# Inputs and output laid out by feature on the host, and a shorter path from the recurrence to the first expert product, in a recurrent mixture-of-experts kernel

## The chip, the cores and the metric

One core of one Trainium2 chip. The metric is the device time of one execution in microseconds (us), the median over the executions shown; lower is better. The profile comes from one further execution of the same program.

## The reference

`x` has the shape (32, 32, 128): 32 rows of 32 time steps with 128 features. A recurrent layer with tanh runs over the 32 steps, and a routed feed-forward layer with 16 experts, top 4 of them per token, works on its states:

```python
xw = einsum('ntd,dh->nth', x, Wx) + b
h_t = tanh(xw_t + h_{t-1} @ Wh)                    # h_0 = cond_1024, 32 steps in series
xn = h * rsqrt(mean(h * h) + 1e-5) * norm_scale
vals, idx = top_k(xn @ wg + bg, 4); gates = softmax(vals), spread to 16 columns
u = xn @ w1[e] + b1[e]                             # (1024 tokens) x 256, for each of 16 experts
s = min(u[::2], 7) * sigmoid(1.702 * min(u[::2], 7)) * (clip(u[1::2], -7, 7) + 1)
out = x + h + sum_e gates[:, e] * (s @ w2[e] + b2[e])
```

## The kernel before, in words

All work runs with features on partitions and tokens in columns. The 1,024 tokens are 8 tiles of 128 columns; a tile is 4 time steps of 32 rows. The tiles form three chunks of 2, 2 and 4 tiles. The experts' work is cut into 32 units: 8 units of 2 experts for chunk 0, 8 such units for chunk 1, 16 units of one expert for chunk 2. A unit has 512 columns of result per half. Order is written out by hand: each engine has its own instruction stream, and semaphores join the streams.

**A unit** (`for v in range(NU)` in every stream). TensorE computes the half `a` into `psA` and the half `b` into `psB` (`up`, L849). Each expert's product has three passes: rounded weights by rounded input (`w1_hi`, `xn_hi`), the weights' rounding rest by rounded input (`w1_lo`, `xn_hi`), and rounded weights by the input's rest (`w1_hi`, `xn_lo`). ScalarE takes `psA` through two activations (L527, L536), VectorE takes `psB` into `lin` (L726) and forms `act` (L741), GpSimd multiplies by the gates (L440), and TensorE adds `w2`'s product four units later (`down`, L878).

**The recurrence** is spread through the same streams. Eight steps form the head, ahead of unit 0; the other 24 run two to a unit in units 0 to 11. Step t is a matmul by `wh_sb` (L798) on top of the product of `x` and `wx` already in PSUM (`x_wx`, L790), then a tanh on ScalarE (L476). The next step waits for it.

**Normalise.** For each group of tiles ScalarE squares (L489), TensorE sums (L805), GpSimd takes the power (L394), TensorE lays the result over the partitions (`lay_rstd`, L820), and VectorE multiplies into `xn` (L587), rounds it to `xn_hi` (L590) and, in the head's two groups, subtracts for `xn_lo` (L594). Then the gates are worked out on VectorE and GpSimd (L610 to L656), turned on TensorE (L838), written to DRAM and read back over all partitions (L339, L345).

**Layout.** `x` comes in with its 32 rows on partitions, `cond` and the two vectors as rows. TensorE transposes them (L779, L917), `b1` as well (L940), and VectorE copies each result out of PSUM (L681 to L686, L697, L745). Tiles 4 to 7 of `x` are transposed in unit 2. At the end of each chunk the result `yT` is transposed back (L901, L911), copied out (L499, L548, L551, L766) and stored in pieces of 32 partitions (L312, L351).

**Fillers.** `keep_warm` (L827) issues matmuls on constants: seven of 512 columns at the start, and some of 256 columns later.

ScalarE also rounds the weights `w1` (L484) in the head from step 2 on and in units 0 to 2; VectorE (L669) and GpSimd (L423) form the rests.

Of the kernel before, what the change touches and what calls it, by code (L numbers as in the profile page):

```python
# [15 lines left out]
def adaln_rnn_moe_kernel(nc, x, cond, wx, wh, b, norm_scale, wg, bg, w1, b1, w2, b2, out):  # L16
# [7 lines left out]
    N, T, D = x.shape  # L24
    E, H, I2 = w1.shape
# [5 lines left out]
    NT = N * T // P  # L31
# [10 lines left out]
    WARM, WARM_START, WARM_GAP = 512, 7, 256  # L42
# [7 lines left out]
    XW_TILES = W // P  # L50
# [12 lines left out]
    ROWS_OUT = [UNIT0[c + 1] + LAG + 2 for c in range(NC - 1)] + [None]  # L63
# [6 lines left out]
    with ctx:  # L70
# [10 lines left out]
        rows = sb("rows", [N + 2, D])  # L81
        wx_sb = sb("wx_sb", [D, H])
        wh_sb = sb("wh_sb", [H, H])
        x_sb = sb("x_sb", [N, T, D])
        b1_sb = sb("b1_sb", [E, I2])
        wg_sb = sb("wg_sb", [H, E])
        bg_sb = sb("bg_sb", [P, E])
        b2_sb = sb("b2_sb", [E, H])
        w1_sb = sb("w1_sb", [H, E, I2])
# [11 lines left out]
        b_col = sb("b_col", [P, 2])  # L101
# [4 lines left out]

        xT = sb("xT", [D, NT * P])
        hT = sb("hT", [H, (T + 1) * N])
# [27 lines left out]
        y_sb = sb("y_sb", [P, NT, D])  # L136
# [5 lines left out]
        rows_loaded = sem("rows_loaded")  # L142
        x0_loaded = sem("x0_loaded")
        x1_loaded = sem("x1_loaded")
        x_loaded = sem("x_loaded")
        wx_loaded = sem("wx_loaded")
        wh_loaded = sem("wh_loaded")
        b1_loaded = sem("b1_loaded")
        wg_loaded = sem("wg_loaded")
# [6 lines left out]
        x_t = sem("x_t")  # L156
        xT_ready = sem("xT_ready")
# [21 lines left out]
        x_mm = sem("x_mm")  # L179
        x_read = sem("x_read")  # L180
# [11 lines left out]
        out_mm = sem("out_mm")  # L192
        rows_ready = sem("rows_ready")
        last_rows = sem("last_rows")
# [5 lines left out]

        out_v = out.rearrange("n (j s) d -> s n j d", s=TL)
        w1_v = w1.rearrange("e h i -> h e i")
        w2_v = w2.rearrange("e i h -> i e h")
# [75 lines left out]
        def xw_bank(j):  # L279

            return psY if j in (0, 2) else psR

        def step_psum(t):

            k = t % (TL * XW_TILES)
            return xw_bank(t // TL)[:, k * N:(k + 1) * N]
# [4 lines left out]
        def psM_turn(what):  # L291

            order = ["rows", "b1"] + [(k, g) for g in range(last_group(0) + 1) for k in ("stats", "rstd")]
# [7 lines left out]
        def psX_turn(what):  # L301

# [12 lines left out]
        def _(sp):  # L315
# [32 lines left out]
            def store_rows(c):  # L348

                for s in range(TL):  # L350
                    sp.dma_start(out_v[s][:, tiles(c), :], y_sb[s * N:(s + 1) * N, tiles(c), :]).then_inc(stored, 16)  # L351
# [676 lines left out]
```

## Time and profile before

| | |
|---|---|
| median of three executions | 113.96 us (113.69 to 113.98) |
| profiled execution: its time, its span | 113.94 us, 112.1 us |
| busy share of TensorE, VectorE, ScalarE, GpSimd | 95%, 59%, 56%, 57% |
| the chain that ended last, by engine | TensorE 84%, VectorE 10%, ScalarE 2% |
| DMA traffic | 12.96 MB, mean 116 GB/s |

The span runs from the first to the last instruction; the 1.84 us between it and the time lie around it. The chain is followed back from the last instruction: at each step to what released it, or to the instruction before it on its engine. So its shares say on which engine time was spent where nothing else could have ended the kernel earlier.

### The profile page before, as it was taken

The page shows a single profiled execution, that of the slowest core. Times are in us where ns is not written, and L with a number is a line of the kernel's source. Part 1 is how long each engine was busy: PE and PEld are TensorE (multiplying, and loading weights), DVE is VectorE, ACT ScalarE, POOL GpSimd, SP SyncE. Part 2 cuts the span into 40 slices and gives each one's busy share as a digit, 9 for nine tenths or more (in the row PEclk, how much of TensorE's full clock was granted, in tenths as well). Part 3 has the DMA queues.
Part 4 walks back from the last instruction along what each step waited for, and adds up shares of the span by engine and source line. Part 5 has one row for each costly group of instructions (what it writes and reads, how often), then busy time and mean ns, then how long its engine had stood idle before and what let it go on. Part 6 is the DMA issues. An engine that isn't in the chain of part 4 may idle for free.

```text
span 112.1 us, 1830 instructions
## 1 busy us (share of the span) xinstructions
PE 106.6 (95%) x600; PEld 90.7 (81%) x600; DVE 66.5 (59%) x180; ACT 62.7 (56%) x143; POOL 64.4 (57%) x76
## 2 busy tenths in 40 slices
PE   7999999999999999999999979999999999999970
PEld 2478978999889999999989968886888888888840
DVE  0110359876735996389756995668265566656720
ACT  4026582998736668567715756654455665466120
POOL 3002444996790698729980799795444575466000
PEclk9999999999999999999999999999999999999999
DMA  1699992007950000992059605990001000000002
GB/s 31 154 268 237 318 303 67 6 9 152 368 231 0 0 6 6 275 371 105 12 129 348 272 6 118 310 368 5 0 0 47 3 0 0 0 0 6 0 23 70
DMA packets 8781, 12.96 MB, mean 116 GB/s; under 512 B 1122, under 2 KB 6628, under 8 KB 8740
## 3 DMA queue, kind: packets, MB, share of 16 engines
q1 hardware_dynamic: 8608, 12.77, 36.4%
q10 hardware_dynamic: 164, 0.07, 0.3%
q8 instruction: 5, 0.08, 0.3%
q14 instruction: 4, 0.03, 0.1%
HBM read 12.25 MB, written 0.59 MB: 114 GB/s over the span
## 4 chain that ended last, share of the span: by engine, by line
PE 84%; DVE 10%; ACT 2%; issue 1%; DVEq 0%
PE psA L849 19%; PE psB L849 18%; PE psY L878 10%; PE psR L878 5%; PE psM L878 5%; PE psR L798 4%; PE psA L827 3%; PE psY L798 2%; PE psB L779 2%; PE psM L805 2%; PE psR L890 2%; PE psM L890 2%; DVE lin L726 1%; PE psR L790 1%; PE psX L838 1%; DVE act L741 1%
## 5 line engine op out<-in xcount | busy, mean ns | idle before, releaser
L440 POOL TENSOR_TENSOR actg<-act,gate_cols 128x512 f32<-128x512 f32 x31 | 39.4, 1282 | 13.8 <-DVE act L741 13.3
L726 DVE TENSOR_SCALAR lin<-psB,one_b1b 128x256 f32<-128x256 f32 (+1 forms) x48 | 25.9, 567 | 22.7 <-PE psB L849 22.7
L527 ACT ACTIVATE psA<-psA,lim_b1a 128x256 f32<-128x256 f32 (+1 forms) x48 | 23.9, 516 | 25.2 <-PE psA L849 25.2
L741 DVE SCALAR_TENSOR_TENSOR act<-lin,psA 128x512 f32<-128x512 f32 x32 | 21.9, 685 | 1.9 <-ACT psA L536 0.6
L536 ACT ACTIVATE psA<-psA,limit_col 128x512 f32<-128x512 f32 x32 | 21.1, 660 | 0.8
L849 PE MATMUL psA<-xn_hi,w_hi 128*128 128x256 f32 (+1 forms) x48 | 20.0, 417 | 0.2 <-DVE xn_hi L590 0.2
L878 PE MATMUL psY<-actg,w_sb 128*128 128x256 f32 x64 | 17.0, 389 | 0.0
L849 PE MATMUL psB<-xn_hi,w_hi 128*128 128x256 f32 (+1 forms) x48 | 16.1, 335 | 0.0
L849 PE MATMUL psA<-xn_lo,w_hi 128*128 128x256 f32 (+1 forms) x48 | 15.6, 325 | 0.0
L849 PE MATMUL psA<-xn_hi,w_lo 128*128 128x256 f32 (+1 forms) x48 | 15.5, 324 | 0.0
L849 PE MATMUL psB<-xn_hi,w_lo 128*128 128x256 f32 (+1 forms) x48 | 15.5, 324 | 0.0
L849 PE MATMUL psB<-xn_lo,w_hi 128*128 128x256 f32 (+1 forms) x48 | 15.5, 322 | 0.0
L423 POOL TENSOR_TENSOR w_lo<-w_sb,w_hi 128x256 fp32r<-128x256 f32 x13 | 9.4, 747 | 10.0 <-ACT w_hi L484 10.0
L878 PEld LDWEIGHTS psY<-actg,w_sb 128*128 128x128 f32 x64 | 11.2, 190 | 1.9 <-issue 0.7
L402 POOL TENSOR_TENSOR expo<-euler,diff 128x6 f32<-128x6 f32 x4 | 5.3, 1326 | 11.4 <-DVE diff L624 11.4
L476 ACT ACTIVATE hT<-psR,b_col 128x32 f32<-128x32 f32 x24 | 6.9, 287 | 8.2 <-PE psR L798 7.9
L849 PEld LDWEIGHTS psA<-xn_hi,w_hi 128*128 128x128 f32 x48 | 9.3, 195 | 1.0 <-issue 0.6
L849 PEld LDWEIGHTS psB<-xn_hi,w_lo 128*128 128x128 f32 x48 | 9.4, 195 | 0.7
L849 PEld LDWEIGHTS psA<-xn_lo,w_hi 128*128 128x128 f32 x48 | 9.3, 194 | 0.7
L798 PEld LDWEIGHTS psR<-hT,wh_sb 128*128 128x128 f32 x48 | 8.8, 209 | 1.4 <-issue 0.5
L849 PEld LDWEIGHTS psB<-xn_hi,w_hi 128*128 128x128 f32 x48 | 9.3, 194 | 0.7
L849 PEld LDWEIGHTS psB<-xn_lo,w_hi 128*128 128x128 f32 x48 | 9.2, 193 | 0.8
(105 smaller groups left out, 148.1 us busy)
## 6 DMA issues: line engine op xcount, KB each, us to landing
gate_cols<-gate_rows SPq DMA_DIRECT2D x16, 512.0 KB, 5.6
w_sb<-in_L_ffn_w SPq DMA_DIRECT2D x4, 512.0 KB, 7.5
w_sb<-in_L_ffn_w SPq DMA_DIRECT2D x4, 256.0 KB, 8.2
out<-y_sb SPq DMA_DIRECT2D x14, 32.0 KB, 1.6
x_sb<-in_x SPq DMA_DIRECT2D x1, 256.0 KB, 5.9
x_sb<-in_x SPq DMA_DIRECT2D x1, 192.0 KB, 2.8
x_sb<-in_x SPq DMA_DIRECT2D x1, 64.0 KB, 2.1
wx_sb<-in_L_cond_Wx SPq DMA_DIRECT2D x1, 64.0 KB, 1.9
```

The source lines that it names most:

```text
L402: nc.gpsimd.tensor_tensor(expo[:, tq, 1:K], euler[:, :, :], diff[:, tq, 1:K], ALU.pow).then_inc(pool_chain, 1)
L423: nc.gpsimd.tensor_tensor(w1_lo[:, pe_, a, :], w1_sb[:, pe_, a::2], w1_hi[:, pe_, a, :].bitcast(F32), ALU.subtract).then_inc(w1_half_ready, 1)
L440: nc.gpsimd.tensor_tensor(by_pair(actg[:, u % SUM_DEPTH, w]), by_pair(act[:, u % ACT_DEPTH, w]), gate_block(u, w), ALU.mult).then_inc(actg ...
L476: nc.scalar.activation(hT[:, (t + 1) * N:(t + 2) * N], step_psum(t), ACT.Tanh, bias=b_col[:, 0:1]).then_inc(step_done, 1)
L527: last = nc.scalar.activation(psA[u % 2][:, o], psA[u % 2][:, o], ACT.Relu, scale=-1.0, bias=lim_b1a[:, e0 + k:e0 + k + 1])
L536: nc.scalar.activation(psA[u % 2][:, 0:w], psA[u % 2][:, 0:w], ACT.Gelu_apprx_sigmoid, scale=-1.0, bias=limit_col[:, :]).then_inc(swish_do ...
L726: last = nc.vector.tensor_scalar(lin[:, v % 2, o], psB[v % 2][:, o], one_b1b[:, e0 + k:e0 + k + 1], LIMIT + 1.0, ALU.add, ALU.min)
L741: nc.vector.scalar_tensor_tensor(act[:, v % ACT_DEPTH, 0:w], lin[:, v % 2, 0:w], 1.0 - LIMIT, psA[v % 2][:, 0:w], ALU.max, ALU.mult).then_ ...
L798: nc.tensor.matmul(step_psum(t), wh_sb[:, :], hT[:, t * N:(t + 1) * N], start=False, stop=True, skip_group_check=True).then_inc(step_mm, 1)
L849: last = nc.tensor.matmul(o, w[:, e0 + k, a, :], x_part[:, cols(c)], start=(m == 0), stop=(m == 2))
L878: last = nc.tensor.matmul(y, w2_sb[:, e0 + k, :], actg[:, u % SUM_DEPTH, a], start=False, stop=(e0 + k == E - 1))
L890: ins = nc.tensor.matmul(y_end_bank(k)[:, 0:PW], w2_sb[:, e0, :], actg[:, u % SUM_DEPTH, o], start=False, stop=(u == NU - 1))
```

## The change

The host now hands the arrays over with features on partitions and joined where they are needed together: `wx_x` is `wx` and the whole of `x`, `small` is `wh`, `b`, `norm_scale`, `b1`, `wg` and `cond`. The output leaves as (128, 1024) and the host turns it. So all transposes of `x`, of the rows, of `b1` and of the output fall away with their copies, and the stores are single pieces. `w1` comes with its two halves apart instead of interleaved.

Besides that: seven opening fillers become five; fillers of 256 columns stand where transposes stood in the head; tiles 3 and 4 of `x` are multiplied by `wx` together at the head's end and tiles 5 to 7 in unit 6, where before tile 3 stood alone and tiles 4 to 7 came in unit 4. In the head's two groups VectorE writes `xn_hi` straight from the product and then computes it once more as `xn`. In the first half of unit 0 the two experts' passes that need only `xn_hi` come first, the two that need `xn_lo` last.

```diff
-    WARM, WARM_START, WARM_GAP = 512, 7, 256
+    WARM, WARM_START, WARM_GAP = 512, 5, 256
...
+    XW_AT = [0, 0, 1, 1, 2, 1, 2, 3]
+    XW_LATE = 5
...
+            sp.dma_start(wx_x_sb[:, 0:H + P], wx_x[:, 0:H + P]).then_inc(wx_x0_loaded, 16)
+            sp.dma_start(wx_x_sb[:, H + P:H + 3 * P], wx_x[:, H + P:H + 3 * P]).then_inc(x1_loaded, 16)
...
+            acte.dma_start(small_h[:, 0:SM], small).then_inc(small_loaded, 16)
...
+            for c in range(NC - 1):
+                sp.wait_ge(yT_ready, c + 1)
+                store(sp, cols(c))
+            for k in range(2):
+                o = slice((NT - 4 + 2 * k) * P, (NT - 2 + 2 * k) * P)
+                sp.wait_ge(yT_ready, NC + k)
+                store(sp, o, slice(0, P) if k == 0 else slice(0, P // 2))
...
+            acte.wait_ge(yT_ready, NC + 1)
+            store(acte, slice((NT - 2) * P, NT * P), slice(P // 2, P))
...
+                if g < CHUNKS[0]:
+                    nc.vector.scalar_tensor_tensor(xn_hi[:, group_cols(g)], h, b_col[:, 1:2], n, ALU.mult,
+                                                   ALU.mult).then_inc(xn_hi_ready, 1)
+                nc.vector.scalar_tensor_tensor(xn[:, group_cols(g)], h, b_col[:, 1:2], n, ALU.mult,
+                                               ALU.mult).then_inc(m_read, 1)
...
+                order = [(k, m) for k in range(r) for m in range(3)]
+                first, end = [(k, 0) for k in range(r)], [(k, 2) for k in range(r)]
+                if u == 0 and a == 0:
+                    order = sorted(order, key=lambda km: km[1] == 2)
+                    first, end = order[:1], order[-1:]
...
             for t in range(HEAD):
                 step(t)
-                if t == 0:
+                if t in (0, 1, 2, TL, TL + 2):
                     keep_warm(2)
-                elif t == 1:
-                    pe.wait_ge(x1_loaded, 16)
-                    transpose_x(1, psB[0], 1).then_inc(x_t, 1)
-                elif t == 2:
-                    transpose_x(2, psB[1], 0)
                 elif t == 3:
                     x_wx(1, 1)
...
                 else:
                     lay_rstd(0)
                     x_wx(2, 1)
+            keep_warm(1)
+            pe.wait_ge(step_done, HEAD)
             sums(1).then_inc(m_mm, 1)
             pe.wait_ge(wg_ready, 1)
             raw_logits(pair_tiles(0), psB[0]).then_inc(raw_mm, 1)
             lay_rstd(1)
-            x_wx(3, 1)
-            keep_warm(1)
+            x_wx(3, 2)
```

## Rows read from the trace of the kernel before

**Rows 1.** The page: TensorE's busy time, and its granted clock in 40 slices

```profile
PE 106.6 (95%) x600; PEld 90.7 (81%) x600; DVE 66.5 (59%) x180; ACT 62.7 (56%) x143; POOL 64.4 (57%) x76
...
PEclk9999999999999999999999999999999999999999
```

**Rows 2.** The chain in order of time: start us, us, what

```profile
0.77 3.15 PE psA L827 x7
...
16.89 0.24 DVE xn_hi L590
...
17.26 1.62 PE psA L849 x6
...
20.57 0.80 PE psA L849 x6
...
24.59 1.11 PE psX L779 x16
...
29.52 0.86 PE psR L790 x2
...
83.67 0.22 PE psX L911 x2
...
108.09 0.43 DVE yT L763
```

**Rows 3.** The timeline of the head: start us, us, engine, line, what

```profile
0.74 0.38 SPq L316 DMA_DIRECT2D rows<-in_cond  x1
...
3.56 0.43 SPq L324 DMA_DIRECT2D w_sb<-in_L_ffn_w  x1
...
5.20 0.76 PE L790 MATMUL psY<-xT,wx_sb 128*128 128x128 f32 x2
...
6.33 0.29 ACT L476 ACTIVATE hT<-psY,b_col 128x32 f32<-128x32 f32 x1 [3.25 <-PE psY L798]
...
7.35 0.29 ACT L476 ACTIVATE hT<-psY,b_col 128x32 f32<-128x32 f32 x1 [0.73 <-PE psY L798]
...
9.04 0.43 ACT L484 ACTIVATE w_hi<-w_sb 128x256 fp32r<-128x256 f32 x1 [0.27 <-DMA w_sb<-in_L_ffn_w]
```

**Rows 4.** DMA issues: what, queue, how many, KB each, median us to landing

```profile
x_sb<-in_x SPq DMA_DIRECT2D x1, 192.0 KB, 2.8
x_sb<-in_x SPq DMA_DIRECT2D x1, 64.0 KB, 2.1
```

**Rows 5.** The timeline from the head's last tanh to unit 0

```profile
13.77 0.29 ACT L476 ACTIVATE hT<-psR,b_col 128x32 f32<-128x32 f32 x1 [0.52 <-PE psR L798]
...
16.26 0.63 PE L790 MATMUL psR<-xT,wx_sb 128*128 128x128 f32 x2
...
16.50 0.35 DVE L587 SCALAR_TENSOR_TENSOR xn<-hT,b_col,psM 128x128 f32<-128x128 f32 x1 [0.31 <-PE psM L820]
16.68 0.42 PE L827 MATMUL psA<-const-bfloat16-1.0 128*128 128x256 bf16 x1
```

**Rows 6.** The timeline of units 2, 3 and 6: steps, tanh and activation

```profile
24.51 0.26 ACT L476 ACTIVATE hT<-psR,b_col 128x32 f32<-128x32 f32 x1
...
25.13 0.66 ACT L536 ACTIVATE psA<-psA,limit_col 128x512 f32<-128x512 f32 x1
...
26.08 0.29 ACT L476 ACTIVATE hT<-psR,b_col 128x32 f32<-128x32 f32 x1 [0.29 <-PE psR L798]
...
35.66 0.30 PE L798 MATMUL psR<-hT,wh_sb 128*128 128x32 f32 x2
...
36.00 0.29 ACT L476 ACTIVATE hT<-psR,b_col 128x32 f32<-128x32 f32 x1 [0.25 <-PE psR L798]
```

**Rows 7.** Who waited for whom, whole span: us in total, times, longest

```profile
PEld psX L838 <- DVE gates L656: 1.0, 2, 0.8
```

**Rows 8.** The stores: the timeline of the tail, and the DMA issues

```profile
109.42 0.88 ACTq L312 DMA_DIRECT2D out<-y_sb  x2
...
out<-y_sb SPq DMA_DIRECT2D x14, 32.0 KB, 1.6
```

More of the change, by code:

```diff
@@ L3, with adaln_rnn_moe_kernel @@
 from contextlib import ExitStack
-def adaln_rnn_moe_kernel(nc, x, cond, wx, wh, b, norm_scale, wg, bg, w1, b1, w2, b2, out):
+def adaln_rnn_moe_kernel(nc, wx_x, small, bg, w1, w2, b2, out):
     F32 = mybir.dt.float32
@@ L30, in adaln_rnn_moe_kernel @@
     TL = P // N
-    NT = N * T // P
+    NT = NTOK // P
     NG = 4
@@ L291, in psM_turn @@
         def psM_turn(what):
-            order = ["rows", "b1"] + [(k, g) for g in range(last_group(0) + 1) for k in ("stats", "rstd")]
+            order = [(k, g) for g in range(last_group(0) + 1) for k in ("stats", "rstd")]
             later = []
@@ L827, in keep_warm @@
                     nc.tensor.matmul(psA[1][:, 0:w], warm[:, 0:P], warm[:, 0:w], start=True, stop=True)
-            def turn_x(what):
-                if psX_turn(what) > 1:
-                    pe.wait_ge(x_read, psX_turn(what) - 1)
             def transpose_gates(q):
                 pe.wait_ge(scale_done, q + 1)
-                turn_x(("gates", q))
+                if q:
+                    pe.wait_ge(gT_ready, q)
                 for k, j in enumerate(pair_tiles(q)):
                     last = nc.tensor.transpose(psX[0:E, k * P:(k + 1) * P], gates[:, j, :], ident[:, :])
-                last.then_inc(x_mm, 1)
+                last.then_inc(gates_mm, 1)
             def up(u, a, bank, done):
                 c, e0, r = unit(u)
-                for k in range(r):
-                    o = bank[:, part(c, k)]
-                    for m, (w, x_part) in enumerate(((w1_hi, xn_hi), (w1_lo, xn_hi), (w1_hi, xn_lo))):
-                        if m == 2 and k == 0 and a == 0 and u == UNIT0[c]:
-                            pe.wait_ge(xn_ready, last_group(c) + 1)
-                        last = nc.tensor.matmul(o, w[:, e0 + k, a, :], x_part[:, cols(c)], start=(m == 0), stop=(m == 2))
+                passes = ((w1_hi, xn_hi), (w1_lo, xn_hi), (w1_hi, xn_lo))
+                order = [(k, m) for k in range(r) for m in range(3)]
[3 more added lines that the diff above has]
+                    first, end = order[:1], order[-1:]
+                for k, m in order:
+                    if m == 2 and k == 0 and a == 0 and u == UNIT0[c]:
+                        pe.wait_ge(xn_ready, last_group(c) + 1)
+                    w, x_part = passes[m]
+                    last = nc.tensor.matmul(bank[:, part(c, k)], w[:, e0 + k, a, :], x_part[:, cols(c)],
+                                            start=((k, m) in first), stop=((k, m) in end))
                 last.then_inc(done, 1)
@@ L979, in _ @@
                     transpose_gates(q)
-                if v == 2:
-                    pe.wait_ge(x_loaded, 16)
-                    turn_x("x")
-                    for j in range(XW_TILES, NT):
-                        last = transpose_x(j, psX, j - XW_TILES)
-                    last.then_inc(x_mm, 1)
                 for q in at(STATS, v):
```

251 lines of the change are left out of this document (70 added, 181 removed).

## The prediction

> **What bounds the kernel now.** I read the page first. TensorE is busy for 95% of the span [rows 1], and the chain that ended last lies on it for 84%; so a microsecond taken from TensorE is a microsecond gained unless something else is late in the same place. Then I read the chain in order of time [rows 2], to find which of the touched lines lie on it, and the timeline around each [rows 3, 5, 6] for what would be late next. The chain shows three kinds of place. In the head (to 17.26 us) the recurrence runs in series: TensorE, ScalarE, TensorE. In units 0 to 3 TensorE leads, but ScalarE is nearly full behind it. From unit 4 on TensorE leads, except where it waits for the gates: two such waits are seen, of 0.2 and 0.8 us [rows 7], at 40.5 and 65 us. The tail is a short series again.
>
> TensorE's clock matters for every number in the head. The page grants it 9 of 10 or more in all slices [rows 1], but the matmuls say otherwise: six matmuls of 256 columns take 1.62 us in unit 0 and 0.80 us in unit 1 [rows 2]. From the start to 20 us the spacing is that of 1.2 GHz (0.213 us for 256 columns), after it that of 2.4 GHz. The rise came 2.74 us after the unbroken run of `up` matmuls began.
>
> **Part 1, the opening: 2.05 us.** Before, `cond` and the vectors are turned and copied, then tile 0 of `x`, and the first `x_wx` starts at 5.20, the first tanh at 6.33 [rows 3], 1.13 later. After, `x_wx` needs five fillers over and the first load landed. The fillers: seven take 3.15 [rows 2], of which five start-to-start are 2.13, so TensorE is free at 2.95. The load is 128 KB, issued first at 0.74 [rows 3]. A 64 KB piece landed 2.1 after its issue, a 192 KB one 2.8 [rows 4]; I take the middle, 2.4, hence 3.15. The `small` load (107 KB, on ScalarE's queue at the same time) gives about 3.0 by the same rows and is wanted only by step 0. So `x_wx` at 3.15 and the first tanh at 4.28: 2.05 gained. Bounds: 2.25 if the load is as quick as 64 KB, and 1.65 if as slow as 192 KB.
>
> **Part 2, the eight steps: 0.30.** The first two tanh are 1.02 apart with two fillers between the steps [rows 3]: step matmuls 0.68 to the tanh, 0.29 tanh, 0.05 to the next. The seven intervals to 13.77 [rows 5] add up to 7.44, because four transposes at a time hold TensorE about 0.1 longer than the tanh does. With two fillers there instead, all seven are 1.02, together 7.14. The `b1` transposes were hidden already and bring nothing. Below nothing it can't go unless a load is late (a rival).
>
> **Part 3, head to unit 0: 0.15.** `xn` took 0.35 from 16.50 and the separate rounding ended the wait at 17.12, unit 0 began at 17.26 [rows 2, 5]. Writing `xn_hi` directly lets it begin 0.27 earlier, at 16.99. But TensorE is not free then: `x_wx` of one tile runs from 16.26 to 16.68 [rows 5], two tiles take twice 0.42 and end at 17.11. So 0.15; bounds 0 and 0.27. The second product makes `xn_lo` about 0.12 later, ready near 17.6; the reordered passes want it four matmuls of 0.213 after 17.11, at 17.96. Without the reordering they would want it at 17.54, so this edit only guards the gain; it brings nothing by itself. VectorE's routing starts 0.1 later, and TensorE wants its gates only in unit 1, over a microsecond after they are ready.
>
> **Part 4, units 2 to 7: 0.68.** Sixteen transposes of 1.11 in all fall out of unit 2 [rows 2]. They do not bring 1.11, since ScalarE is next. Step 13 could start once tanh 12 (24.51 to 24.77) is over, near 24.84 instead of 25.70; its own tanh stood at 26.08 but must follow the activation of 25.13 to 25.79 [rows 6], so it moves only to 25.82. What ScalarE then does (two roundings of `w1`, two activations, two tanh) is back to back through unit 3, so 0.26 arrives at step 15. In unit 4 the `x_wx` of four tiles, 0.86 for 512 columns [rows 2], is gone: 1.12 ahead. In unit 6 three tiles, 0.64, come back: TensorE is 0.48 ahead. The gates, on VectorE from unit 5's activation, keep the 1.12. TensorE waited 0.2 for them [rows 7], and of that wait nothing is left: 0.48 + 0.20 = 0.68 gained at unit 7. Bounds: 0.26 if ScalarE's lag is passed on whole and the late `x_wx` holds up unit 6, and 1.3 (1.11 and 0.21 for the tile moved to the head) if nothing else is in the way.
>
> **Part 5, the chunks' ends: 0.22.** The transposes of chunk 1's result lie on the chain, 0.22 at 83.67 [rows 2]. Chunk 0's run at 62.9, ahead of the 0.8 wait for the gates [rows 7]: worth 0. The VectorE and ScalarE copies were off the chain: 0.
>
> **Part 6, the tail: 0.22 + 1.30.** Two transposes between the last `down` matmuls, at 106.97, go: one more row like that of 83.67, again 0.22 [rows 2]. The last `yT` add ends at 108.51 [rows 2]; the first of the last four stores is issued at 109.42 and each queue issues two, the second near 109.9 [rows 8]. After, each queue issues one store 0.05 after the add: 1.3 earlier. A 32 KB store landed 1.6 after its issue [rows 8]; the new ones are 64 KB, and by the loads' rows a larger piece may take 0.3 more, so 1.0 to 1.3.
>
> A page of the Trainium skill, DMA: Bandwidth & Descriptors, section Rules for kernel authors, speaks against the split of that last store over two queues: disjoint partition halves share the same 16 DMA engines. By it the split is worth nothing against one store, and an estimate with the landing of a 128 KB piece like that of the loads would make the tail 0.4 worse. No row of before shows two such halves.
>
> **Part 7, `w1`'s layout: 0.** ScalarE, VectorE and GpSimd read it with unit stride now. ScalarE's rounding of 256 strided columns took 0.43 [rows 3], its activation of 512 contiguous ones 0.66 [rows 6]: 0.23 for 256 columns and 0.20 fixed explain the 0.43 without any cost of the stride, so no gain in duration. Larger pieces may bring `w1` in earlier, which matters only for the rival below.
>
> **Sum.** 2.05 + 0.30 + 0.15 + 0.68 + 0.22 + 0.22 + 1.30 = 4.92 us. It is made against the profiled execution, 113.94, which is the median less 0.02: 109.0 us. Its own range is 108.1 to 109.9, from the bounds of the parts.
>
> **Rivals.** *The clock rises in the head.* Five times two fillers of 256 columns now stand where transposes and waits stood. If the rise comes at about the fourth step, a step costs 0.34 less (step matmul to tanh 0.34 at high clock [rows 6] against 0.68), four of them 1.35; sums and raw logits give about 0.4; unit 0's first half 0.8, after which ScalarE leads. Together 2.5: 106.5. Against it: seven fillers of 512 columns did not raise the clock. Chance 0.17. The Trainium skill, TensorE: Matmul & The Clock Gate, section Part 4, says that transposes do not count as busy for the clock. By that rule the head after, almost free of them, is the kind that raises it; the trace agrees in so far as the head with transposes stayed at 1.2 GHz to the end.
>
> *The clock stays low longer.* If the rise stays at 20.0 of the trace instead of following unit 0, which now starts at 14.76, TensorE works 2.5 us more at 1.2 GHz and loses half, 1.25, of which ScalarE's lag would have cost 0.2 anyway: 110.0. For it: there are fewer opening fillers. Chance 0.15.
>
> *A load is late.* ScalarE waits in order for `w1` between tanh 2 and tanh 3. `w1` landed 5.5 after its issue at 3.56 [rows 3]; issued at 1.63 it would come at 7.1, and tanh 3 wants it by 6.85. With a late first load, 0.4 more: 109.3 to 109.8. Chance 0.10.
>
> *Slower.* The low clock lasts. To eat 4.92 and 0.34 more at half a microsecond for each, it must last 10.5 us longer than 2.74 after unit 0 began, to 28 us. That gives 114.3 or more. No wait of TensorE for the gates is over 0.8 [rows 7], and none of these lowered the clock. Chance 0.02. *Transposes were free anyway*, that is only the opening and the tail count: 113.94 less 3.6, 110.4, chance 0.03.
>
> **How the numbers follow.** The forecast has 0.53, the clock early 0.17, late 0.15, a late load 0.10, slower 0.02, free 0.03. The likeliest gives 109.0. The range of 106.8 to 110.3 holds all but part of the early clock, the slow case and half of the last. Faster or slower here means by over 0.3%, or 0.34 us, what this kernel's measurement can tell: faster 0.97, same 0.01, slower 0.02.
>
> **What would show it.** The first tanh near 4.3, the eighth near 11.4, unit 0's first matmul near 14.8 with spacing 0.213, the rise near 17.5; tanh 13 right behind an activation; no wait of TensorE for the gates in unit 7, a wait of 0.8 or more near 60; the last stores issued within 0.1 of the last add. A rise before 12 us or after 19 makes it wrong, as does a ScalarE idle for `w1` in the head.

## The result and the profile after

The kernel before took 113.97 us in this measurement (113.69 to 114.84, 4 executions), the changed one 112.31 (110.01 to 114.59, 4 executions). The changed kernel's four executions took 110.0, 110.2, 114.4 and 114.6; the ratio is formed without the two long ones and is 0.965 with an interval of 0.956 to 0.974, which is 110.0 us. The profiled execution took 110.22 with a span of 108.4; that of the kernel before took 113.94 with 112.1. The forecast was 109.0, so 3.7 us of span came out of 4.92 forecast.

The page of the changed kernel, TensorE's busy time and its granted clock:

```profile
PE 102.9 (95%) x562; PEld 87.0 (80%) x562; DVE 64.6 (60%) x173; ACT 60.8 (56%) x139; POOL 63.8 (59%) x76
...
PEclk9999999999999999999999999999999999999999
```

The timeline of the changed head (start, duration, engine, line, what; in brackets the idle time before it and what ended it):

```profile
3.33 0.80 PE L714 MATMUL psY<-wx_x_sb 128*128 128x128 f32 x2 [0.27 <-DMA wx_x_sb<-in_wx_x]
4.49 0.29 ACT L441 ACTIVATE small_h<-psY,small_h 128x32 f32<-128x32 f32 x1 [1.82 <-PE psY L722]
...
7.39 0.42 ACT L449 ACTIVATE w_hi<-w_sb 128x256 fp32r<-128x256 f32 x1 [0.58 <-DMA w_sb<-in_w]
...
11.75 0.29 ACT L441 ACTIVATE small_h<-psR,small_h 128x32 f32<-128x32 f32 x1 [0.42 <-PE psR L722]
...
12.02 0.35 DVE L538 SCALAR_TENSOR_TENSOR xn_hi<-small_h,psM 128x128 fp32r<-128x128 f32 x1 [1.43 <-PE psM L744]
...
12.28 0.34 DVE L540 SCALAR_TENSOR_TENSOR xn<-small_h,psM 128x128 f32<-128x128 f32 x1
...
12.77 0.56 PE L729 MATMUL psM<-ones,sq 128*128 128x1 f32 x2
...
15.22 0.55 PE L774 MATMUL psA<-xn_hi,w_hi 128*128 128x256 f32 x1
```

The first tanh is 1.84 us ahead of that of before (6.33 in [rows 3]), the eighth 2.02 (13.77 in [rows 5]), unit 0's first matmul 2.04 (17.26 in [rows 2]). So up to unit 0 the head gives 2.04 of the 2.50 forecast: 0.21 is missing in the opening, 0.12 in the steps, where ScalarE stands 0.58 for the load of `w1` (its rounding at 7.39) ahead of tanh 3, and 0.13 between the last tanh and unit 0.

Units 0 and 1 then lose 0.76 of it again (2.04 at unit 0, 1.28 at unit 2). The timeline of the changed kernel where TensorE's clock rises, in unit 1:

```profile
19.42 0.41 PE L774 MATMUL psA<-xn_hi,w_hi 128*128 128x256 f32 x1
19.63 0.41 PE L774 MATMUL psA<-xn_hi,w_lo 128*128 128x256 f32 x1
19.84 0.34 PE L774 MATMUL psA<-xn_lo,w_hi 128*128 128x256 f32 x1
...
20.36 0.28 PE L774 MATMUL psB<-xn_hi,w_lo 128*128 128x256 f32 x1
20.48 0.28 PE L774 MATMUL psB<-xn_lo,w_hi 128*128 128x256 f32 x1
```

Starts are 0.21 apart until 19.84 and 0.12 apart from 20.36 on. The rise of TensorE's clock to 2.4 GHz comes at 19.95, where it was at 20.0 before, although unit 0 starts two microseconds sooner: 4.7 us after unit 0's first matmul instead of 2.74. The page's row of the granted clock shows 9 all along and can't be used for this; the spacing of the matmuls can. Unit 2's first matmul stands at 21.31 against 22.59, which is 1.28 ahead.

The timeline of units 2 and 7 of the changed kernel, steps, activation, tanh and the gates' transposes:

```profile
23.54 0.41 PE L722 MATMUL psR<-small_h 128*128 128x32 f32 x2 [0.19 <-ACT small_h L441]
23.84 0.66 ACT L492 ACTIVATE psA<-psA,limit_col 128x512 f32<-128x512 f32 x1
...
24.43 0.28 ACT L441 ACTIVATE small_h<-psR,small_h 128x32 f32<-128x32 f32 x1
...
38.44 0.38 PE L758 MATMUL psX<-ident,gates 128*16 128x128 f32 x2
```

Tanh 13 (24.43) follows the activation without a pause, as forecast; the step's own matmuls (23.54) waited 0.19 for ScalarE's tanh 12. How far TensorE is ahead of the kernel before, by the starts of the same instructions in both timelines:

| place | before | after | ahead |
|---|---|---|---|
| unit 2, first `up` | 22.59 | 21.31 | 1.28 |
| unit 3, first `up` | 25.88 | 23.79 | 2.09 |
| unit 4, first `up` | 27.86 | 26.15 | 1.71 |
| unit 4, step 16, behind the `x_wx` of before | 30.22 | 27.66 | 2.56 |
| unit 6, first `up` | 35.97 | 33.41 | 2.56 |
| unit 7, first `up`, behind the `x_wx` of after | 38.70 | 36.79 | 1.91 |
| unit 7, gates' transposes | 40.56 | 38.44 | 2.12 |

The steps of this table are the terms of part 4 one by one: 0.43 for the transposes of `x` from unit 2 to unit 4 (0.26 forecast; 0.81 of lead at unit 3, of which ScalarE takes 0.38 back), 0.85 for four tiles of `x_wx` (0.86), -0.65 for three (-0.64), 0.21 for the wait (0.20). Units 2 to 7 gave 0.84. Who waited for whom in the changed kernel (us in total, times, longest):

```profile
PEld psX L758 <- DVE gates L609: 1.2, 2, 1.0
...
POOL actg L406 <- DMA gate_cols<-gate_rows: 0.8, 1, 0.8
...
PEld psY L804 <- POOL actg L406: 0.3, 1, 0.3
```

TensorE no longer waits for the gates in unit 7; the two waits left are a new one in unit 11 (0.2, at 50.8 us) and the one ahead of the transposes at 63.2 (1.0). In their place a wait in unit 4 appears that I had not named: GpSimd stands 0.8 for the gate columns, which go through DRAM, and TensorE 0.3 behind it. By the table it cost nothing in this execution.

The chain of waits at the end of chunk 1 no longer has the two transposes (0.22 in [rows 2]). The tail of the changed kernel, from its timeline and from the waits of SyncE's queue:

```profile
104.05 2.19 SPq L292 DMA_DIRECT2D out<-yT  x2
105.26 0.42 DVE L701 TENSOR_TENSOR yT<-wx_x_sb,psM 128x256 f32<-128x256 f32 x1 [1.24 <-PE psM L816]
105.71 0.56 ACTq L292 DMA_DIRECT2D out<-yT  x1
```

```profile
SPq L72 <- DMA out<-yT: 1.8, 1, 1.8
```

The last add ends at 105.68, 2.83 ahead of before, and the span ends 2.72 later, where before it was 3.6 (108.51 to 112.1): the tail's stores give 0.87. The store is issued 0.03 after the add's end, as forecast. But from the issue of the last store to the end of the span 2.69 go by (105.71 to 108.4), where before it was 2.24 (109.86 to 112.1, the second of two issues of 0.44 from 109.42): this 0.45 is what is missing of the 1.30. The whole: 2.04 - 0.76 + 0.84 + 0.22 + 0.22 + 0.27 + 0.87 = 3.7. The 0.27 is what is left of the 2.83 after the two pairs of transposes, and I had not forecast it. None of it comes before unit 20: by their first `up`, unit 19 is 2.11 ahead, unit 22 2.19, unit 24 2.43 (chunk 1's transposes lie between) and unit 31 2.58. In units 25 to 31 a unit takes about 2.24, and before 2.26.

### The profile page after: what moved, and what is told of

It is laid out like the page before. It is cut to its first block, busy times and chain, and to the rows that moved or that the text cites. A ratio compares the mean times of both kernels' runs of the same rounds, so it can differ in the third digit from the quotient of the medians.

```text
span 108.4 us, 1718 instructions
## 1 busy us (share of the span) xinstructions
PE 102.9 (95%) x562; PEld 87.0 (80%) x562; DVE 64.6 (60%) x173; ACT 60.8 (56%) x139; POOL 63.8 (59%) x76
## 4 chain that ended last, share of the span: by engine, by line
PE 79%; DVE 9%; ACT 5%; DMA 2%; issue 1%; DVEq 0%
PE psA L774 19%; PE psB L774 17%; PE psY L804 10%; PE psR L804 5%; PE psR L722 5%; PE psM L804 5%; PE psY L722 2%; DMA wx_x_sb<-in_wx_x 2%; PE psA L751 2%; PE psM L729 2%; PE psR L714 2%; ACT psA L483 2%; PE psR L816 2%; ACT psA L492 2%; PE psM L816 2%; DVE lin L667 1%
## 5 line engine op out<-in xcount | busy, mean ns | idle before, releaser
L492 ACT ACTIVATE psA<-psA,limit_col 128x512 f32<-128x512 f32 x32 | 21.1, 660 | 0.8
L774 PE MATMUL psA<-xn_hi,w_hi 128*128 128x256 f32 (+1 forms) x48 | 20.5, 428 | 0.0
L441 ACT ACTIVATE small_h<-psR,small_h 128x32 f32<-128x32 f32 x24 | 6.9, 286 | 7.6 <-PE psR L722 7.3
L722 PEld LDWEIGHTS psR<-small_h 128*128 128x128 f32 x48 | 8.8, 210 | 2.7 <-ACT small_h L441 1.9
L774 PEld LDWEIGHTS psA<-xn_hi,w_lo 128*128 128x128 f32 x48 | 9.7, 202 | 0.5
```

Source lines behind the costliest of these rows:

```text
L441: nc.scalar.activation(hT[:, (t + 1) * N:(t + 2) * N], step_psum(t), ACT.Tanh, bias=b_col[:, 0:1]).then_inc(step_done, 1)
L492: nc.scalar.activation(psA[u % 2][:, 0:w], psA[u % 2][:, 0:w], ACT.Gelu_apprx_sigmoid, scale=-1.0, bias=limit_col[:, :]).then_inc(swish_do ...
L722: nc.tensor.matmul(step_psum(t), wh_sb, hT[:, t * N:(t + 1) * N], start=False, stop=True, skip_group_check=True).then_inc(step_mm, 1)
L774: last = nc.tensor.matmul(bank[:, part(c, k)], w[:, e0 + k, a, :], x_part[:, cols(c)], start=((k, m) in first), stop=((k, m) in end))
```

## The experiments

Five things were open. When does the clock rise, and what did its lateness cost? Where did the 0.13 between tanh and unit 0 go? What are the moved `x_wx` and the new order of the passes worth? What is the tail's split worth? What is the new wait in unit 4? The runs follow in that order. Where the text says "unit 0", its first `up` matmul is meant; "rise" is the time at which starts go from 0.21 apart to 0.12.

**again**: the changed kernel unchanged, to see how far it repeats.

> The changed kernel unaltered, as the reference point for the others. If the time at which TensorE goes from 1.2 to 2.4 GHz is tied to the start of the program, the rise comes again near 20.0 us of the span, as in both traces so far (between 19.96 and 20.15 before, between 19.84 and 20.02 after), and the profiled span is 108.2 to 108.6 us. If it falls at random, this run's rise lies elsewhere between 15 and 24 us and its span moves by half of the shift.

It took 110.75 us (109.13 to 112.33, 4 executions), ratio 0.963 [0.954, 0.971]. So its executions, here and in the result, lie between 109.1 and 111.0, and three of eight above that. In the profiled execution (span 109.2) the first load landed later, so that `x_wx` began at 4.39 instead of 3.33 and unit 0 at 16.14; the rise came at 20.4. So the landing of the first load and the rise both vary, the first by 1.1 us between two executions of one kernel. The rise is not tied to 20.0 us, nor to unit 0 by a fixed distance.

**warm9**: nine opening fillers, four more, by which `x_wx` waits for TensorE and no longer for the load.

```diff
-    WARM, WARM_START, WARM_GAP = 512, 5, 256
+    WARM, WARM_START, WARM_GAP = 512, 9, 256
```

> Nine opening fillers instead of five: TensorE is free at 4.61 us and the first x_wx starts there instead of at 3.33, everything up to unit 0 is 1.28 us later. Theory A (the rise stays at 20.0 us of the trace): the 1.28 us of delay only push work from low to high clock, the span grows by about 0.6 (109.0). Theory B (the rise follows the unbroken run of up matmuls by a fixed 4.7 us): rise near 21.3, span 109.7. Theory C (more columns early raise the clock early): rise before unit 0, span under 107.5.

It took 109.46 us (108.31 to 110.06), ratio 0.954 [0.947, 0.962], although `x_wx` starts at 4.57. Its page and its timeline:

```profile
PEclk9995555999999999999999999999999999999999
```

```profile
5.41 0.29 ACT L441 ACTIVATE small_h<-psY,small_h 128x32 f32<-128x32 f32 x1 [2.73 <-PE psY L722]
...
6.19 0.29 ACT L441 ACTIVATE small_h<-psY,small_h 128x32 f32<-128x32 f32 x1 [0.50 <-PE psY L722]
...
9.57 0.29 ACT L441 ACTIVATE small_h<-psR,small_h 128x32 f32<-128x32 f32 x1 [0.53 <-PE psR L722]
```

The clock is up in the opening, a step takes 0.78 instead of 1.02, and it falls at 8.4, ahead of the sixth tanh: the one before 9.57 stands at 8.55, 1.02 earlier. Now that a fall follows a rise the page shows it, as 5 in four slices. Unit 0 begins at 15.07, 0.15 sooner than in the changed kernel in spite of the later opening, and the rise in unit 1 comes at 18.7. The fillers are therefore no pure cost; they buy fast steps, as long as the clock holds. None of the three theories had a rise followed by a fall.

**kw3**: three fillers instead of two between the head's steps, five fillers in the opening.

```diff
-                    keep_warm(2)
+                    keep_warm(3)
```

> Three fillers of 256 columns instead of two at five places between the head's steps. TensorE then holds each of these steps to 0.42 + 0.64 = 1.06 us instead of 1.02, about 0.2 us longer in all. Theory A (the rise is tied to 20.0 us): span 108.6. Theory C (denser streaming in the head raises the clock before unit 0): from then on a step costs 0.34 us less and unit 0 runs at 2.4 GHz, span 106 to 107.

It took 109.54 us (107.25 to 113.98). No rise in the head; unit 0 at 15.05, rise at 18.9, span 108.1. The third filler costs nothing, where 0.2 was expected: the tanh are 1.01 to 1.02 apart, as with two. But it did not bring the clock up in this execution.

**norm0**: only group 1, the one that unit 0 waits for, writes `xn_hi` directly; group 0 does as before.

```diff
-                if g < CHUNKS[0]:
+                if g == 1:
                     nc.vector.scalar_tensor_tensor(xn_hi[:, group_cols(g)], h, b_col[:, 1:2], n, ALU.mult,
                                                    ALU.mult).then_inc(xn_hi_ready, 1)
...
-                if g >= CHUNKS[0]:
+                if g != 1:
                     nc.vector.tensor_copy(xn_hi[:, group_cols(g)], xn[:, group_cols(g)]).then_inc(xn_hi_ready, 1)
```

> Only the head's second group writes xn_hi directly; the first group goes back to product, rounding, rest. Theory: in the changed kernel the release of psM (m_read) stands on the second product of group 0 (12.28 to 12.62 us), and the sums of group 1 wait for it until 12.77; with one product first it comes 0.26 us earlier, the sums start at about 12.5 (bound by the square, ready at 12.38), unit 0 starts 0.2 to 0.26 us earlier, at 15.0. Of it half to all shows in the span (108.1 to 108.3), since TensorE is at 1.2 GHz there. Rival: the sums wait for something else (the filler issued ahead of them), then nothing moves.

It took 108.99 us (108.91 to 109.54), ratio 0.957 [0.952, 0.962]. Its timeline at the same place:

```profile
11.68 0.29 ACT L441 ACTIVATE small_h<-psR,small_h 128x32 f32<-128x32 f32 x1 [0.42 <-PE psR L723]
...
11.95 0.35 DVE L540 SCALAR_TENSOR_TENSOR xn<-small_h,psM 128x128 f32<-128x128 f32 x1 [1.43 <-PE psM L745]
...
12.45 0.56 PE L730 MATMUL psM<-ones,sq 128*128 128x1 f32 x2
...
14.91 0.55 PE L775 MATMUL psA<-xn_hi,w_hi 128*128 128x256 f32 x1
```

`sums(1)` writes the bank `psM` that group 0's normalise reads, and waits for `m_read`. In the changed kernel `m_read` hangs on the second product (12.28 to 12.62) and `sums(1)` starts 1.02 after the last tanh; here it hangs on the first and only one, and `sums(1)` starts 0.77 after it. That is the 0.25 that group 1's direct write had gained: 3.23 from tanh to unit 0 here, 3.47 in the changed kernel (3.49 in *again*, 3.48 in kw3), 3.49 before. The rise came at 17.5, 2.5 after unit 0 instead of 4.7. The span is 107.2, 1.2 less than that of the changed kernel. Of this 0.31 is unit 0's earlier start (0.24 by the edit, 0.07 by the steps); the other 0.9 goes with 2.2 us less at the low clock, which by itself would be 1.1. All four executions had spans of 107.1 to 107.7. Whether the edit brings the earlier rise or it fell so by chance is not shown.

**xwold**: `x_wx` as before the change (tile 3 in the head, tiles 4 to 7 in unit 4), all else changed.

```diff
-    XW_AT = [0, 0, 1, 1, 2, 1, 2, 3]
-    XW_LATE = 5
+    XW_AT = [0, 1, 2, 3, 0, 1, 2, 3]
+    XW_LATE = 4
...
-            x_wx(3, 2)
+            x_wx(3, 1)
+            keep_warm(1)
```

> The changed kernel with the products x wx as before: tile 3 alone at the head's end with one filler behind it, tiles 4 to 7 in unit 4. Theory: nothing changes at the head's end (two tiles take 0.85, one tile and a filler 0.64 and then a wait for xn_hi; unit 0 at most 0.1 earlier); in unit 4 step 16 comes 0.86 later, in unit 6 nothing is inserted; at unit 7 the gates' wait is back (0.2 or more) and TensorE stands where it stood in the changed kernel plus or minus 0.25. Rival: the move to unit 6 is worth the full 0.64.

One execution, 110.63 us, span 108.8. Unit 2 begins 0.21 later than in the changed kernel (21.52), but unit 3 begins at 23.76 against 23.79 there: the step between the two waits for ScalarE in both kernels, and this takes the difference up. Step 16 is 0.84 later (28.50 against 27.66), behind the four tiles of `x_wx`; the gates' transposes in unit 7 are 0.40 later (38.84 against 38.44), with a wait of 0.2 for the gates that the changed kernel does not have. The terms of part 4 give 0.86 - 0.64 + 0.20 = 0.42 for the same edit. I had expected no more than 0.25 at unit 7. It is one execution, but both starts are compared behind a place where the two kernels stand level.

**noreorder**: unit 0's passes in the common order, each expert's `xn_lo` pass behind its two others.

```diff
-                if u == 0 and a == 0:
+                if False:
```

> The changed kernel without the new order of passes in unit 0: the third matmul of unit 0 wants xn_lo, which is ready 0.65 us after xn_hi (15.07 to 15.66 in the changed trace). It could start at 15.79 at 1.2 GHz with the old order, so theory: a wait of under 0.1 us at the third matmul, the first half of unit 0 ends within 0.1 us of before; the reordering is worth 0 to 0.1 us. Rival: it is worth the 0.3 us that a wait for xn_lo from a third matmul at 15.5 would cost.

One execution, 112.29 us, span 110.5. At unit 0 the order is worth 0.1: the unit starts at 15.13, 0.09 sooner than in the changed kernel, its third matmul is held up by `xn_lo`, and the second half begins at 16.92 in both. What made this execution long is elsewhere. Its waits, its clock in the middle of chunk 0's units, and its page:

```profile
28.59 2.49 POOL L406 TENSOR_TENSOR actg<-act,gate_cols 128x512 f32<-128x512 f32 x2 [1.40 <-DMA gate_cols<-gate_rows]
...
29.91 0.75 PEld L804 LDWEIGHTS psY<-actg,w_sb 128*128 128x128 f32 x4 [0.76 <-POOL actg L406]
```

```profile
28.00:30.00 2.00, 1.64 (x12) 1.22 (x11) 1.73 (x5) 1.09 (x3) 1.41 (x2) 1.00 1.02 354
30.00:32.00 2.00, 2.00 (x8) 1.77 (x9) 0.00 (x0) 0.29 (x1) 2.00 (x3) 0.64 0.55 223
32.00:34.00 2.00, 2.00 (x12) 2.00 (x11) 0.00 (x0) 0.81 (x2) 1.00 (x1) 0.50 0.02 8
34.00:36.00 2.00, 2.00 (x16) 1.90 (x16) 1.50 (x4) 1.13 (x3) 0.00 (x0) 1.00 0.00 0
```

```profile
PEclk9999999999958999999999999999999999999999
```

The second fence is a table by stretch: the stretch, its length, then busy time and number of instructions of PE, PEld, DVE, ACT and POOL, the granted clock, the DMA share and GB/s. GpSimd stood 1.40 for the gate columns, TensorE's weight load 0.76 for GpSimd, and right behind it the clock is 0.64 and then 0.50 for two stretches, with 12 matmuls in 2 us where 16 stand in the next. The wait of unit 4 has grown here by 0.6 and is followed by 3.4 us at 1.2 GHz (0.36 and 0.50 of two stretches of 2 us lacking, divided by a half), which costs 1.7 of the 2.1 us that this span is longer. The starts agree: at unit 4's first `up` this execution is 0.09 behind the changed kernel's, at unit 6's 2.08, and 2.07 to 2.09 from there to the end. The run of **onestore** below shows the same: a wait of 1.34 for the gate columns, one of 0.71 at TensorE's weight load at 29.60, and 3.4 us at the low clock by the same sum (0.50 and 0.65 granted). It is 0.16 ahead of the changed kernel at unit 4 and 1.79 behind at unit 6.

**early**: chunk 0's gates are turned in the middle of unit 1 and copied ahead of ScalarE's second activation there, so that the columns are laid out in time.

```diff
                         for t in steps_at(u, 0):
                             tanh(t)
+                        if u == 1:
+                            copy_gates(0)
...
                 for q in at(GATES_T, u):
-                    copy_gates(q)
+                    if q:
+                        copy_gates(q)
...
                     for t in steps_at(v, 0):
                         step(t)
+                    if v == 1:
+                        transpose_gates(0)
...
                 for q in at(GATES_T, v):
-                    transpose_gates(q)
+                    if q:
+                        transpose_gates(q)
```

> The changed kernel with the gates of chunk 0 turned and copied right behind step 10, in the middle of unit 1, and not at its end: the copy ends near 21.3 us instead of 22.35, so the gate columns arrive about 1 us earlier. Theory: in the changed kernel the x transposes and the four-tile product no longer cover the columns' way through DRAM; GpSimd waited 0.8 to 1.4 us for them and TensorE 0.3 to 0.8 at its first down of unit 4, and in the run without reordering a wait of 0.8 was followed by matmuls at 1.2 GHz from 29.9 to 34. With the earlier start GpSimd's wait is under 0.3, TensorE's is gone, and no run is over 111.5 us, where the changed kernel had 114.4 and 114.6. Rival: the long runs have another cause, then about one in four stays over 111.5.

It took 110.1 us (109.21 to 110.4, 7 executions), ratio 0.969 [0.964, 0.974]. In its waits the one for the columns is down from 0.8 to 0.2, and TensorE's in unit 4 is gone:

```profile
POOL actg L406 <- DMA gate_cols<-gate_rows: 0.2, 1, 0.2
```

The copy starts at 19.77 instead of 21.99; of this about 1.0 is the edit, for in norm0, where the clock rises equally early, it starts at 20.79. The time is that of the changed kernel's shorter executions, and the spread is small: 1.2 us over seven executions, where the changed kernel's eight went from 109.1 to 114.6. That fits with the fall of the clock behind this wait as the cause of the long executions, but it is not shown. The two traces above have the fall in neighbours of the changed kernel, none has it in the kernel itself; and norm0, warm9 and dense, which leave the gates where they were, had nothing above 110.1 in four executions each.

**dense**: norm0, nine opening fillers, four between steps, and more beside `x_wx`, the sums and the raw logits, to keep the clock up to unit 0.

```diff
-    WARM, WARM_START, WARM_GAP = 512, 5, 256
+    WARM, WARM_START, WARM_GAP = 512, 9, 256
...
-                    keep_warm(2)
+                    keep_warm(4)
                 elif t == 3:
                     x_wx(1, 1)
+                    keep_warm(2)
                 elif t == TL + 1:
                     pe.wait_ge(consts_ready, 1)
                     sums(0).then_inc(m_mm, 1)
+                    keep_warm(2)
...
-            keep_warm(1)
+            keep_warm(3)
...
+            keep_warm(2)
             lay_rstd(1)
```

> The run with nine opening fillers had its matmuls at 2.4 GHz spacing from 4.7 to 8.6 us and a step of 0.78 instead of 1.02, then fell back until 18.7. Here: nine opening fillers, four fillers of 256 columns instead of two between steps, two more behind the head's other inserts, three and two around the sums and raw logits of group 1, and the first group's normalise in the old order. Theory C (columns streamed decide): the clock is up at 4.7 and stays up; eight steps take 0.8 each, unit 0 starts near 12.5 and runs at 2.4 GHz, span 104.5 to 106. Rival: the clock falls all the same, then each step costs 1.27 at 1.2 GHz, unit 0 starts near 17 and the span is 108.5 or more.

It took 108.03 us (107.88 to 108.23), ratio 0.945 [0.938, 0.952], span 106.3. The early rise came as expected; unit 0 near 12.5 and a span of 104.5 to 106 did not. From the first step on the clock stays up; steps take 0.78, but for one held up by `w_hi`; unit 0 begins at 14.15 although `x_wx` started only at 4.56, at the high clock. The timeline of dense between units 0 and 2:

```profile
18.00 0.87 DVE L668 TENSOR_SCALAR lin<-psB,one_b1b 128x256 f32<-128x256 f32 x2
...
18.90 0.69 DVE L683 SCALAR_TENSOR_TENSOR act<-lin,psA 128x512 f32<-128x512 f32 x1
...
19.73 0.36 PE L775 MATMUL psA<-xn_hi,w_hi 128*128 128x256 f32 x1 [0.87 <-DVE act L683]
```

Unit 2's first matmul waits 0.87 for unit 0's `act`, and that waited for VectorE, which was busy with the routing until about 18 and took `lin` only then. It starts 1.58 sooner than in the changed kernel, where unit 0 started 1.07 sooner: four half units at the high clock bring 0.5 and no more, because VectorE is next.

**dense_early**: both. 

> The run with dense fillers, with the gates of chunk 0 turned in the middle of unit 1 as well. There TensorE's waits were for act of unit 0 (ahead of unit 2), not for the gate columns, so the earlier gates give little: 107.6 to 108.1 us against 107.9 to 108.2. Rival: the copy placed ahead of the second activation holds ScalarE up in its full stretch and costs 0.2 to 0.4.

It took 108.01 us (107.51 to 108.43, 6 executions), ratio 0.949 [0.943, 0.954], span 106.3: nothing over dense, whose wait for the gate columns was only 0.3.

**before_out**: the kernel before, with nothing of the change but the output's layout, its stores, and the dropped transposes and copies of the output.

```diff
-            rows_end(1)
...
+            acte.wait_ge(yT_ready, NC + 1)
+            store(acte, slice((NT - 2) * P, NT * P), slice(P // 2, P))
```

> The kernel before with one part of the change alone: the output is laid out by feature, its transposes and copies are gone, and the four stores of the changed kernel stand in their place. Theory: this part does not depend on the clock's rise; it brings what the changed trace shows for it, 0.22 for chunk 1's transposes, 0.22 before the last add and 0.87 behind it, together 1.3 us (span 110.8, time 112.6). Rival: part of the 3.7 us of the whole change that looks like tail comes from elsewhere, then it brings under 1.0.

It took 112.42 us (112.02 to 113.46) against 114.02, ratio 0.985 [0.976, 0.994]; span 110.8. The last add ends at 108.06, 0.45 ahead of before, and the end is 2.74 behind it instead of 3.6: 0.86 for the stores. Of the 0.45 the tail's transposes give 0.22, those of chunk 1 0.17 (0.06 ahead at unit 22, 0.23 at unit 31), and 0.06 comes from the head, which is not as it was although nothing in it is changed. Its page and two of its first tanh:

```profile
PEclk9985555699999999999999999999999999999998
```

```profile
6.49 0.29 ACT L463 ACTIVATE hT<-psY,b_col 128x32 f32<-128x32 f32 x1 [0.50 <-PE psY L768]
7.27 0.29 ACT L463 ACTIVATE hT<-psY,b_col 128x32 f32<-128x32 f32 x1 [0.50 <-PE psY L768]
```

After the same seven fillers as before, and with the transposes of `x` between the steps, the clock is up here: the tanh are 0.78 apart, until the granted clock falls at 7.4. Unit 0 begins at 16.42, 0.84 sooner than before. But the clock rises again only at 21.1, 4.7 after unit 0, and by unit 2 just 0.11 of the lead is left (22.48 against 22.59). So an early rise that does not last brought next to nothing, and whether it comes differs between executions. A mean granted clock as low as this trace's 0.934, between 0.93 and 0.96, is on record for ten of 37 further executions of the kernel before (nine took 113.6 to 114.3 us, one 112.6) and for two of eight of the changed one; that these are early rises too is my reading, no trace of them is kept.

**onestore**: the changed kernel with its last store as one piece on SyncE's queue.

```diff
-                store(sp, o, slice(0, P) if k == 0 else slice(0, P // 2))
+                store(sp, o)
...
-            acte.wait_ge(yT_ready, NC + 1)
-            store(acte, slice((NT - 2) * P, NT * P), slice(P // 2, P))
```

> The changed kernel with the last 128 KB stored by one issue of SyncE instead of two halves from SyncE and ScalarE. By the Trainium skill, DMA: Bandwidth & Descriptors, section Rules for kernel authors, halves on two queues share the same engines and one transfer is no worse. Theory from rows: from the last add's end to the span's end it took 2.7 us with halves; the 128 KB store ahead of it landed 1.7 to 2.0 after its issue, so one store ends within 0.2 us of two. Rival: the halves are worth 0.3 us or more, as 192 KB against 64 KB at the loads would say.

One execution, 111.39 us, span 109.6, with the fall of the clock told under noreorder. Its tail does not depend on that. Timeline, and waits of SyncE's queue:

```profile
105.81 1.99 SPq L292 DMA_DIRECT2D out<-yT  x2
107.02 0.42 DVE L699 TENSOR_TENSOR yT<-wx_x_sb,psM 128x256 f32<-128x256 f32 x1 [1.24 <-PE psM L814]
```

```profile
SPq L72 <- DMA out<-yT: 1.4, 1, 1.4
```

From the end of the last add (107.44) to the end of the span 2.16 us go by, with two halves 2.72; SyncE's issues end 0.2 sooner and the wait for the landing is 0.4 shorter. The split costs 0.56, where I had expected 0.2 at most and, as the rival, a gain by it. It is one execution, but not luck: all eleven traces with halves have 2.69 to 2.74 there, and the other one with a single store (**best**) has 2.11. The DMA issues (KB each, median us to landing) show why, the two halves of the changed kernel first, then the stores of onestore:

```profile
out<-yT SPq DMA_DIRECT2D x1, 64.0 KB, 2.0
out<-yT ACTq DMA_DIRECT2D x1, 64.0 KB, 2.3
...
out<-yT SPq DMA_DIRECT2D x4, 128.0 KB, 1.7
```

**best**: dense_early with the one store. 

> All that the runs point to, together: nine opening fillers and the denser ones, the first group's normalise in the old order, the gates of chunk 0 turned in the middle of unit 1, and one last store. Theory: the store's gain of 0.5 (2.16 us from the last add's end to the span's end, against 2.7 with halves) adds to the 108.0 of the dense kernels, so 107.5, with all executions between 107.0 and 108.0. Rival: the 0.5 was the luck of one trace, then it stays at 108.0 and the tail of this trace takes 2.7 again.

It took 107.26 us (106.65 to 107.34, and one execution of 193.5; before 114.02, 11 executions), ratio 0.937 [0.932, 0.943], span 105.3, with 2.11 from the last add to the end. It is the fastest of all, some 2.7 us below the changed kernel. Against dense_early its span is 1.0 shorter: 0.58 is the store, and unit 0 begins 0.39 sooner (13.79), since no step of its head is held up.

The clock over the runs, all at 1.2 GHz up to the rise named (warm9 and before_out after a first high stretch):

| run | unit 0 | rise | rise after unit 0 | span |
|---|---|---|---|---|
| before | 17.26 | 20.0 | 2.7 | 112.1 |
| after | 15.22 | 19.95 | 4.7 | 108.4 |
| again | 16.14 | 20.4 | 4.3 | 109.2 |
| before_out | 16.42 | 21.1 | 4.7 | 110.8 |
| warm9 | 15.07 | 18.7 | 3.6 | 107.7 |
| kw3 | 15.05 | 18.9 | 3.8 | 108.1 |
| norm0 | 14.91 | 17.5 | 2.5 | 107.2 |
| early | 15.13 | 17.2 | 2.1 | 107.4 |
| xwold | 15.11 | 20.5 | 5.4 | 108.8 |
| dense | 14.15 | up before | - | 106.3 |

## Why the prediction was right, and where its gain was too high

**The opening (2.05, came 1.84).** Mechanism right: `x_wx` waits for the load, the fillers are over. The load landed 2.55 after its issue instead of 2.4, and `x_wx` to tanh took 1.16 instead of 1.13. The bounds of 1.65 to 2.25 held, but *again* (0.77 gained) shows the landing can be 1.1 later still; two rows of other sizes were too little to bound it.

**The steps (0.30, came 0.18).** The rival "a load is late" came in part: ScalarE's 0.58 for `w1` held tanh 3 up. The other intervals are the 1.02 of the forecast, in this trace.

**Head to unit 0 (0.15, came 0.02).** The failed step is "writing `xn_hi` directly lets it begin 0.27 earlier": I followed it for group 1 alone. Group 0's second product holds `psM` 0.25 longer, and `sums(1)` was ready for the bank. norm0 shows it: undo group 0's part, and the 0.25 returns. The forecast that TensorE is busy with `x_wx` of two tiles until then held.

**The clock (taken as free, cost 0.76 by unit 2, about 0.9 in all).** This is the largest error, and the step that failed is that the rise follows unit 0, the assumption under part 3's start of unit 0 and part 4's 1.11. It was drawn from one execution, in which 2.74 us was a distance and not a law. Over the runs of the table the rise comes 2.1 to 5.4 us behind unit 0's start and at no fixed time either (17.2 to 21.1), with the same `up` matmuls ahead of it. The rival "the clock stays low longer" named the rise at 20.0 and got it to 0.05 us, which was luck (20.4 in *again*, 17.5 in norm0); it priced the loss at 1.05, where 0.76 came by unit 2. norm0 is the nearest to the forecast's own case, with unit 0 at 14.91 and the rise at 17.5, 2.5 behind it; its span is shorter than the changed kernel's by 0.9 beyond what its unit 0 starts sooner. So about 0.9 is what the late rise cost. The rival "the clock rises in the head" did not come in the traces with five opening fillers and came with nine (warm9, dense). Its ground against, that seven fillers did not raise the clock, was the luck of one trace: in before_out they did. The Trainium skill, TensorE: Matmul & The Clock Gate, Part 4, says that transposes do not count as busy for the clock the way matmuls do. No run here tries this alone: the changed kernel and kw3, almost free of transposes, stayed at 1.2 GHz through the head, and before_out, with them, had 2.4 GHz up to 7.4 us.

**Units 2 to 7 (0.68, came 0.84).** Right, term by term in the table of the result, and for the moved `x_wx` and the gates' wait in xwold too (0.40 for 0.42). Only the transposes of `x` gave 0.43 instead of 0.26, between places on either side of ScalarE's full stretch. Why they gave more is open. That TensorE came to unit 2 with 0.76 less of a lead can't be all of it, for norm0 with more of a lead gained still more there (0.83 ahead of the changed kernel at unit 2, 1.20 at unit 4). In norm0 ScalarE's records follow each other without a pause from unit 0 through unit 3; in the changed kernel it stands 0.23 and 0.47 in unit 1, while TensorE is at the low clock. At unit 7 the changed kernel is 0.6 short of the forecast beyond its later unit 0: the late clock's 0.9, less the 0.3 by which these units were sized too low (norm0 gains 0.97 from unit 0 to unit 7, where 0.68 was forecast).

**Chunk ends and transposes of the tail (0.22 + 0.22).** Right to 0.05, also in before_out (0.17 and 0.22).

**The tail's stores (1.30, came 0.87).** The issue came 1.3 earlier as forecast; the term that was mis-sized is the landing. The sum had it as 1.6, that of a 32 KB store, with at most 0.3 more for the size; the two halves took 2.0 and 2.3. Size is not it, since whole pieces of 128 KB landed after 1.7. The Trainium skill, DMA: Bandwidth & Descriptors, Rules for kernel authors, says not to bother with two transfers to disjoint partition halves, since they share the same engines, and to use one of 128 partitions. onestore and best agree: the halves cost 0.56 against one store. With one store the gain over before would have been 1.44.

**Not forecast.** The 0.27 between unit 7 and the end: its cause stays open, no run was made for it. before_out does not have it (0.06 ahead at unit 22 as at unit 7, and from unit 24 on it falls back by 0.03), so it is not the output's part; `w1`'s layout, which part 7 put at nothing, is among what is left. And the wait for the gate columns in unit 4. It can be seen before: GpSimd waited 0.6 there, with nobody behind it. Units 2 and 3 have less for TensorE to do now, the transfer keeps its length, and so GpSimd's wait grows to 0.8 to 1.4 and reaches TensorE. In the profiled execution it cost nothing; where the clock fell behind it (noreorder, onestore) the run lost 2.0 between units 4 and 6.

## What to carry to other kernels

Look at what else hangs on the semaphore of an instruction that is moved behind another: a release that comes 0.25 later holds up whoever wants the buffer, even in another group. Work taken from the leading engine uncovers the next wait, here a round trip through DRAM, and the table of waits before already has it as a small entry of an engine that nobody waited for. Take the rise of a clock from several executions, not from one, and if fillers are to hold it, put in enough to raise it and keep them up to the first long stretch of matmuls. Store a last piece whole: halves of 64 KB landed later than 128 KB in one.

## What was not expected of the hardware

With nine fillers of 512 columns in the opening the clock was up by the second step in every trace (warm9, dense, dense_early, best). With seven it was in one trace (before_out) and not in the other (before), and with five in none of eight. With two fillers of 256 columns a step it fell back at 8.4 us (warm9), with four it did not (dense). A rise that was lost again at 7.4 us left 0.1 us of lead at unit 2 (before_out).

The page's granted clock reads 9 of 10 from the start even while 256 columns take 0.21 us. In these traces it shows 1.2 GHz only after a first rise, as in warm9 and noreorder; the spacing of matmuls is the safer measure.

A wait of 0.71 to 0.76 of TensorE at 29 to 30 us was followed by 3.4 us at 1.2 GHz (noreorder, onestore); one of 0.6 at the same place (kw3) and one of 1.0 ahead of the gates' transposes at 63.2 us (the changed kernel) were not. So the length of a wait alone does not tell.

The same load of 128 KB, issued at the same time, landed 2.55 us after its issue in one execution and 3.6 in another.
